# Third to fifth sparse product of a graph network: the dense steps of a block run between the next blocks

## Reference

```python
# layer 0: two graph convolutions (first and second sparse product)
# layer 1: one sum over the edges, then two dense layers with a norm over the nodes
agg = jax.ops.segment_sum(x[src] + edge_feat, dst, num_segments=x.shape[0])
h = (1.0 + epsilon) * x + agg
h = jax.nn.relu(_batchnorm(h @ W1 + b1, g1, beta1))
h = jax.nn.relu(_batchnorm(h @ W2 + b2, g2, beta2))
...
# layer 2: two of these, with a leaky ReLU between them
msg = jax.ops.segment_sum(h[src], dst, num_segments=n_nodes)
h_neigh = (msg + h) / (deg[:, None] + 1.0)
return h_neigh @ W + b
...
# layer 3: three rounds that need max, min, mean and variance over the edges of a node
# between the layers
x = _layernorm(x + layer(x), axis=-1)
```

## Time and profile before

| | |
|---|---|
| median of 3 runs | 3185.71 us (3182.45 to 3189.19) |
| profiled execution, its own time | 3187.43 us |
| its span | 3185.6 us |
| busy in the span | PE 2330.5, PEld 1326.7, DVE 2185.1, ACT 659.8, POOL 1274.1 us |
| third product | 844.06 to 953.8 us of the span |
| fourth | 1014.72 to 1118.9 us |
| fifth | 1142.82 to 1246.1 us |
| layer 3, three rounds | from about 1279 us to the end |

### The profile page before, as it was taken

One profiled execution on the slowest core, in us unless ns is written; L12 is line 12 of the kernel. 1 busy time (PEld: TensorE's weight loads), 2 busy tenths in 40 slices (PEclk: granted clock), 3 DMA queues, 4 the chain that ended last, 5 costly groups with the idle time before them and its releaser, 6 DMA issues.

```text
span 3185.6 us, 49509 instructions
## 1 busy us (share of the span) xinstructions
PE 2330.5 (73%) x11826; PEld 1326.7 (42%) x11873; DVE 2185.1 (69%) x6856; ACT 659.8 (21%) x1425; POOL 1274.1 (40%) x1321
## 2 busy tenths in 40 slices
PE   7999869998896988766566767666667676666681
PEld 3444335674563655433333444333334443333351
DVE  8998777557427244766666787666668876666786
ACT  0345551342103010300000043111111421111112
POOL 4000000000200000577777706777775077777740
PEclk9999989999897999878777789777778887777795
DMA  3123347536641543665565406665663166656521
GB/s 134 62 103 124 145 163 258 182 112 216 210 166 64 194 146 113 199 196 196 196 198 194 145 10 227 194 197 194 195 198 114 60 208 196 197 192 197 193 79 41
DMA packets 151716, 510.46 MB, mean 160 GB/s; under 512 B 32178, under 2 KB 51280, under 8 KB 150720
## 3 DMA queue, kind: packets, MB, share of 16 engines
q1 hardware_dynamic: 94254, 348.65, 31.3%
q0 software_dynamic: 43536, 93.43, 11.1%
q10 hardware_dynamic: 13826, 67.12, 5.2%
HBM read 278.95 MB, written 230.13 MB: 160 GB/s over the span
## 4 chain that ended last, share of the span: by engine, by line
PE 28%; DVE 24%; issue 16%; POOL 14%; DMA 11%; ACT 3%; DVEq 2%; ACTq 0%; POOLq 0%
POOL rows_g L671 14%; PE psum L1680 11%; DMA rows_g<-a_dram,idx_now 9%; PE psum L1620 8%; DVE run L853 4%; DVE run L1158 3%; DVE run L1155 2%; PE psum L1913 2%; DMA at_part<-part_now 2%; PE psum L1629 1%; DVE var_tmp L1097 1%; PE psum L1891 1%; PE psum L1752 1%; DVE hs L1204 1%; PE psum L1761 1%
## 5 line engine op out<-in xcount | busy, mean ns | idle before, releaser
L671 POOL DMA_INDIRECT rows_g<-a_dram,idx_now x1173 | 1138.8, 971 | 974.7 <-DMA a_dram<-g 618.1
L1680 PE MATMUL psum<-hs,slab 128*128 128x384 bf16 x6600 | 1174.2, 340 | 55.5 <-DVE hs L835 52.0
L1680 PEld LDWEIGHTS psum<-hs,slab 128*128 128x128 bf16 x6600 | 672.3, 102 | 581.7 <-issue 189.7
L1155 DVE SCALAR_TENSOR_TENSOR run<-run,mask_pt,rows_g 128x128 f32<-128x128 f32 x1170 | 406.0, 347 | 374.9 <-DMA rows_g<-a_dram,idx_now 330.5
L1158 DVE SCALAR_TENSOR_TENSOR run<-run,mask_pt,rows_g 128x128 f32<-128x128 f32 x1170 | 403.6, 345 | 0.1
L1851 PE MATMUL psum<-identity,std_now 128*128 128x128 f32 x75 | 33.9, 452 | 483.8 <-ACT std_now L1513 483.8
L1620 PE MATMUL psum<-onehot_key,onehot_lane 128*128 128x512 bf16 (+1 forms) x1921 | 347.6, 335 | 10.6 <-issue 8.0
L782 DVE TENSOR_SCALAR onehot_key<-key_row,key_at 128x1600 bf16<-128x1600 f16 x492 | 310.1, 630 | 0.0
L1513 ACT ACTIVATE std_now<-var_now,eps 128x128 f32<-128x128 f32 x75 | 30.1, 401 | 1242.7 <-DVE var_now L1117 1242.7
L1620 PEld LDWEIGHTS psum<-onehot_key,onehot_lane 128*128 128x128 bf16 x1968 | 157.3, 98 | 185.6 <-DVE onehot_key L782 20.3
L1851 PEld LDWEIGHTS psum<-identity,std_now 128*128 128x128 f32 x75 | 13.3, 178 | 509.8 <-ACT std_now L1513 509.3
(11 more groups left out here) (319 smaller groups left out, 2742.0 us busy)
## 6 DMA issues: line engine op xcount, KB each, us to landing
slab<-at_part SPq DMA_DIRECT2D x200, 800.0 KB, 4.6
scan_dram<-run SPq DMA_DIRECT2D x291, 512.0 KB, 2.9
at_part<-part_now ACTq DMA_DIRECT2D x50, 800.0 KB, 4.0
sums_dram<-run ACTq DMA_DIRECT2D x43, 576.0 KB, 2.8
rows_g<-a_dram,idx_now POOLq DMA_INDIRECT x1173
rows_g<-in_attr SPq DMA_DIRECT2D x43, 148.5 KB
a_dram<-g SPq DMA_DIRECT2D x15, 320.0 KB, 2.5
agg<-sel_dram SPq DMA_DIRECT2D x3, 1600.0 KB, 8.4
```

The lines of the kernel that those rows point to most:

```text
L671: nc.gpsimd.indirect_dma_start(rows_g[:, slot, j, :], None, a_dram, bass.IndirectOffsetOnAxis(ap=idx_now[:, slot, j:j + 1], axis=0)).then_ ...
L1155: V.scalar_tensor_tensor(at[:, 0:D], before[:, 0:D], mark, rows, ALU.add, ALU.max).then_inc(s_run, 1)
L1680: T_.matmul(ps[:, 0:3 * D], counts[:, k * P:(k + 1) * P], hs[:, k, at:at + 3, :].rearrange("p s f -> p (s f)"), start=(k == 0), stop=False ...
```

## The change

For the third to fifth product the two phases are put into one loop. `with_products` is the loop of TensorE: after the sums of block b come the transpose of block b-1 and the dense product of block b-2. Bank 3 + r % 3 holds the transpose of block r in its first 128 columns and the product in the next 128; `turned` gets three places (`turned_at`). ScalarE copies the turned block in `copy_turned`, between its other work. VectorE runs `behind(b)` after it has taken block b: the result of block b-3, and what follows it up to the split (`leaky_and_split`) or to the normalised rows (`layer_out`), for one to three blocks behind that. The leaky ReLU, the split and the last norm are now done by blocks of 128 rows, and no longer by groups of five or for all 25 at once. The loops are written out: all 25 blocks of a product are instructions of their own, where before they were three of a loop and four or one outside it. The queue of the loads is not changed.

```diff
@@ -83,6 +83,7 @@
 GT = -(-T // Q)
 RING = 4
 PAIRS = -(-NB // 2)
+FINISHED = {2: 7 * NB, 3: 9 * NB, 4: 11 * NB}
...
+        def turned_at(b):
+            return turned[:, b % 3 // 2, b % 3 % 2 * P:b % 3 % 2 * P + P]
...
-                    in_turn(dve, 3, take)
+                    for b in range(NB + late):
+                        if b < NB:
+                            take(b, b % 3, b // 3)
+                        behind(b)
...
+            def result_of(base, r, take):
+
+                dve.wait_ge(s_mm, base + (r + 1))
+                take(r, bank(3 + r % 3)[:, P:2 * P]).then_inc(s_res, 1)
+                dve.wait_ge(s_res, base + (r + 1))
+
+            def first_hidden(b):
+
+                r = b - 3
+                if r >= 0:
+                    result_of(NB, r, lambda r, ps: V.tensor_scalar(blk(ft, r), ps, cols[:, 0:1], None, ALU.add))
+                    if r % (CB // P) == CB // P - 1 or r == NB - 1:
+                        ins_ = chunk_stats(ft, r // (CB // P))
+                        if r == NB - 1:
+                            step(ins_)
+
             gather_sums(2, plus(edge_sum),
                         lambda b, rows: V.scalar_tensor_tensor(rows, row(x, b), one_eps[:, 0:1], rows,
-                                                               ALU.mult, ALU.add))
+                                                               ALU.mult, ALU.add),
+                        behind=first_hidden, late=3)
             dve.sem_inc(s_rows, 1)
-            for i in range(NCB):
-                for b in range(i * CB // P, min(NB, (i + 1) * CB // P)):
-                    dve.wait_ge(s_mm, NB + (b + 1))
-                    V.tensor_scalar(blk(ft, b), bank(4 + b % 2)[:, 0:D], cols[:, 0:1], None, ALU.add).then_inc(s_res, 1)
-                dve.wait_ge(s_res, NB + (b + 1))
-                last = chunk_stats(ft, i)
-            step(last)
...
-            gather_sums(3, plus(x), times(rdeg))
-            dve.sem_inc(s_rows, 1)
-            results(3 * NB + 7, NB, lambda b, ps: V.tensor_tensor(g[:, b, :], ps[:, 0:D], rows3[:, 1, :], ALU.add))
-            dve.wait_ge(s_res, 4 * NB + 7)
-            for i in range(NG):
-                rows = g[:, GB * i:GB * i + GB, :]
-                V.scalar_tensor_tensor(rows, rows, 0.01, rows, ALU.mult, ALU.max).then_inc(s_group, 1)
-            groups_done[0] += NG
-            dve.wait_ge(s_group, groups_done[0])
-            dve.sem_inc(s_rows, 1)
-            split(3, g, 0)
-            gather_sums(4, plus(g), times(rdeg))
-            dve.sem_inc(s_rows, 1)
-            for b in range(NB):
-                dve.wait_ge(s_mm, 4 * NB + NCB + b + 1)
-                V.tensor_tensor(agg[:, b, :], bank(4 + b % 2)[:, 0:D], rows3[:, 2, :], ALU.add).then_inc(s_res, 1)
-                dve.wait_ge(s_res, 4 * NB + NCB + b + 1)
-                step(V.tensor_tensor(agg[:, b, :], agg[:, b, :], x[:, b, :], ALU.add))
-                last = V.bn_stats(stats[:, b, :], agg[:, b, :])
-            step(last)
-            layer_norm(None, 6)
-            by_groups(normalized(x, agg))
+            ahead = NB // 3 + 1
+
+            def leaky_and_split(b):
+
+                r = b - 3
+                if 0 <= r < NB:
+                    result_of(3 * NB + NCB, r, lambda r, ps: V.tensor_tensor(g[:, r, :], ps, rows3[:, 1, :], ALU.add))
+                    V.scalar_tensor_tensor(g[:, r, :], g[:, r, :], 0.01, g[:, r, :], ALU.mult, ALU.max).then_inc(
+                        s_ln_x, 1)
+                r = b - 4
+                if 0 <= r < NB:
+                    dve.wait_ge(s_ln_hi, ahead + r + 1)
+                    V.tensor_tensor(agg[:, r, :], g[:, r, :], hs[:, r, 3, :], ALU.subtract).then_inc(s_ln_rest, 1)
+                r = b - 5
+                if 0 <= r < NB:
+                    dve.wait_ge(s_ln_mid, ahead + r + 1)
+                    V.tensor_tensor(hs[:, r, 5, :], agg[:, r, :], hs[:, r, 4, :], ALU.subtract).then_inc(s_ln_lo, 1)
+
+            gather_sums(3, plus(x), times(rdeg), behind=leaky_and_split, late=5)
+            dve.wait_ge(s_ln_lo, ahead + NB)
+            dve.sem_inc(s_r1, NG)
+            dve.sem_inc(s_hs, NG)
+            dve.sem_inc(s_rows, 2)
+
+            def layer_out(b):
+
+                r = b - 3
+                if 0 <= r < NB:
+                    result_of(4 * NB + NCB, r, lambda r, ps: V.tensor_tensor(agg[:, r, :], ps, rows3[:, 2, :], ALU.add))
+                    step(V.tensor_tensor(agg[:, r, :], agg[:, r, :], x[:, r, :], ALU.add))
+                    step(V.bn_stats(stats[:, r, :], agg[:, r, :]))
+                    V.bn_aggr(mv[:, r, :], stats[:, r, :]).then_inc(s_ln_stats, 1)
+                r = b - 4
+                if 0 <= r < NB:
+                    dve.wait_ge(s_ln_std, ahead + r + 1)
+                    step(V.reciprocal(rstd[:, r:r + 1], std[:, r:r + 1]))
+                    V.tensor_scalar(x[:, r, :], agg[:, r, :], mv[:, r, 0:1], rstd[:, r:r + 1], ALU.subtract,
+                                    ALU.mult).then_inc(s_ln_x, 1)
+
+            gather_sums(4, plus(g), times(rdeg), behind=layer_out, late=4)
+            dve.wait_ge(s_ln_x, ahead + 2 * NB)
+            dve.sem_inc(s_rows, 3)
...
+            def copy_turned(b, trs, mms):
+
+                act.wait_ge(s_tr, trs + (b + 1))
+                if b >= 3:
+                    act.wait_ge(s_mm, mms + (b - 2))
+                A.copy(turned_at(b), bank(3 + b % 3)[:, 0:P]).then_inc(s_trc, 1)
+
             act.wait_ge(s_sel_copy, NG)
-            in_turn(act, 3, sel_block)
-            turned_blocks(NB, NB, NB, D)
+            for i in range(NB + 2):
+                if i < NB:
+                    sel_block(i, i % 3, i // 3)
+                if i >= 2:
+                    copy_turned(i - 2, NB, NB)
             root_of(8, cstd[:], cmv[:, 1:2], 0)
             act.wait_ge(s_rows, 9)
             for i in range(7):
@@ -1471,10 +1519,28 @@
                              scale=cscale[:, 0:1]).then_inc(s_trc, 1)
             root_of(12, std[:], mv[:, :, 1], 0)
             split(2, x, 0, groups=NG)
-            turned_blocks(2 * NB, 3 * NB, 3 * NB + 7, D)
-            split(3, g, 0, groups=2 * NG)
-            turned_blocks(3 * NB, 4 * NB, 4 * NB + 7, D)
-            root_of(17, std[:], mv[:, :, 1], 0)
+            ahead = NB // 3 + 1
+            for i in range(NB + 3):
+                if i < NB:
+                    copy_turned(i, 2 * NB, 3 * NB + NCB)
+                r = i - 2
+                if 0 <= r < NB:
+                    act.wait_ge(s_ln_x, ahead + r + 1)
+                    A.copy(hs[:, r, 3, :], g[:, r, :]).then_inc(s_ln_hi, 1)
+                r = i - 3
+                if r >= 0:
+                    act.wait_ge(s_ln_rest, ahead + r + 1)
+                    A.copy(hs[:, r, 4, :], agg[:, r, :]).then_inc(s_ln_mid, 1)
+            act.sem_inc(s_hi, NG)
+            act.sem_inc(s_mid, NG)
+            for i in range(NB + 2):
+                if i < NB:
+                    copy_turned(i, 3 * NB, 4 * NB + NCB)
+                r = i - 2
+                if r >= 0:
+                    act.wait_ge(s_ln_stats, ahead + r + 1)
+                    A.activation(std[:, r:r + 1], mv[:, r, 1:2], ACT.Sqrt, bias=eps[:, 0:1]).then_inc(s_ln_std, 1)
+            act.sem_inc(s_std, 1)
...
-                    count_products(pe, [bank(slot)], [3 if c == 2 else 0], slab[slot], range(NB - 1), flag, c, b, slot,
-                                   halves)
+                    count_products(pe, [bank(slot)], [3 if c in (2, 4) else 0], slab[slot], range(NB - 1), flag, c, b,
+                                   slot, halves)
 
                 def first():
                     one(0, 0, 0, n)
@@ -1675,7 +1741,10 @@
             def count_products(pe, banks, ats, counts, ks, flag, c, b, slot=0, halves=None):
                 for k in ks:
                     if halves is not None and k % GB == 0:
-                        pe.wait_ge(s_hs, NG * halves + k // GB + 1)
+                        if c == 4:
+                            pe.wait_ge(s_ln_lo, NB // 3 + 1 + k + GB)
+                        else:
+                            pe.wait_ge(s_hs, NG * halves + k // GB + 1)
...
+            def with_products(c, one, first, trcs, ress, product):
+
+                for b in range(NB + 2):
+                    if b == 0 and first:
+                        first()
+                    elif b < NB:
+                        one(b, b % 3, b // 3)
+                    if 1 <= b <= NB:
+                        r = b - 1
+                        pe.wait_ge(s_fin, FINISHED[c] + 2 * r + 2)
+                        if r >= 3:
+                            pe.wait_ge(s_res, ress + (r - 2))
+                        T_.transpose(bank(3 + r % 3)[:, 0:P], agg[:, r, :], identity[:]).then_inc(s_tr, 1)
+                    if b >= 2:
+                        r = b - 2
+                        pe.wait_ge(s_trc, trcs + (r + 1))
```

(24 more changed lines are left out.)

4 lines of the change are left out of this document (2 added, 2 removed).

## The result

The changed kernel takes 3154.3 us (median of 4 runs, 3151.55 to 3155.27) where the kernel before took 3185.15 on the same chip (4 runs, 3182.45 to 3189.19). The ratio is 0.9901, 95% interval [0.9884, 0.9918], so the change saves 30.9 us.

What follows compares the result with a forecast made beforehand. TensorE alone bounds a product, a chain over all engines the stretch between two. Gains of 6.1, 10.8 and 20.3 us at the three ends, net of the products' cost, sum to 37.2: forecast 3149 us, range 3137 to 3165.

Steps and rivals of the forecast that it cites:

- The price of a product: Third to fifth product: the added transposes and dense products lengthen each by 7.4 us, 22.1 in all.
- The rival by which TensorE pays more: Three products: an f32 pair costs 0.47 us, above the distances between starts, 9.5 us more, 3158 us; chance 0.14.
- lockstep: Products: VectorE and ScalarE set the pace, 5 us a block in two products, 30 us lost, 3179 us; chance 0.04.
- The third's end: After the third product: aggregate 3.6 us after its last sum instead of 17.1; 13.5 gained, 6.1 after the product's cost.
- The fourth's end: Fourth product's end to the fifth's block 0: T + 11.3 instead of T + 29.5, gain 10.8 us after the product's cost.
- T: The end of a product's last sum, about 0.02 us before VectorE starts on the last block.
- The 1.75 us for the clock: Fifth product's first block: its slowdown by the reduced clock, 5.65 us instead of 3.9, was kept in the forecast.
- the last split: After the fourth product: block 24's split ready at T + 8, after five late VectorE turns of 1.35 us.
- The fifth's end: After the fifth product: last `take_g` at T + 16.4 instead of T + 44.1, gain 20.3 us after the product's cost.
- one group of them is now ahead, 1.1 us: T + 6.4 + 10.0: Fifth product's end: with one group ahead, the 11.1 us chain to the last `take_g` takes 10.0 after the last result.
- All after the last `take_g` is left as it was: Behind the fifth product's end: nothing changes, gathers start when `g` is in DRAM, nothing else known to hold them.
- Code loading: Written-out blocks: rival that some 20 more instruction packets cost 2.6 us each, 52 us in all, 3200 us; chance 0.06.

Runs made afterwards that it cites:

- Early slabs: The changed kernel with the fifth product's slabs loaded as places come free in the fourth: ratio 0.9905 to the kernel before, fourth's end 7.49 us against 11.35.
- tail kernel: The changed kernel with layer 3's first transposes and copies between the fifth product's late blocks, dense products in banks 5 to 7: ratio 0.9906 to the kernel before.
- the second pair: The kernel before and the changed kernel, both unedited, profiled again on another chip in the last group: medians differ by 31 us.
- the written-out loops: The kernel before with only TensorE's loops of the third to fifth product written out: 3726.02 us, ratio 0.9999 to the kernel before.

## Why the prediction was right, and where it was off

**The price of a product** was right: 7.54, 7.47 and 7.55 us against 7.4. The distances 0.10 and 0.23, read from the earlier trace rows where the work stood in bunches and from the one f32 matmul in the earlier trace rows, held between bf16 sums as 0.11 and 0.22. The rival by which TensorE pays more is refuted by the table, and lockstep by VectorE's 45 us of 103.

**The third's end** was right: 4.06 us for 3.6, a gain of 13.0 for 13.5.

**The fourth's end** was right in size and in cause: T + 11.1 for T + 11.3, the slab used at T + 5.3 for 5.4, the block at mean clock 0.70. The 1.75 us for the clock took the length of a row (5.65) against 24 distances between starts (3.9); length against length (4.07 in the earlier trace rows) it is 1.6, and 1.7 were measured. Early slabs confirmed that the slab's wait, and with it the clock, is what is left. One part was off without effect: the last split came at T + 5.8, not T + 8, since a late turn of VectorE lasts 0.93 us and not 1.35. Had it been 8 the early slabs would have gained less than they did.

**The fifth's end** is the mis-sized term: 18.28 us against T + 16.4, a gain of 25.8 for 27.7, still inside its bounds (T + 14 to T + 20). The last result was even early (T + 5.9 for 6.4), and the last `x` at T + 7.7 for 8.3. The step that failed is "one group of them is now ahead, 1.1 us: T + 6.4 + 10.0". The group's transposes were ahead, but its copy was not: it stood behind three square roots on ScalarE, and the products of the first group began at 1243.32, T + 7.7, where the step has them at about T + 7.5 (6.4, and 1.1 of the 2.2 us between 1279.08 and 1281.26 in the earlier trace rows). From there the chain took 10.5 us until the last take, against 8.9 from 1281.26 to 1290.20: the half clock, taken by the sum as over after ten transposes, lasted from 1241.6 until about 1248 and covered the five products of the first group (2.50 us) and the transposes of the third group (1.27 for five) as well. The tail kernel, which has the copies between the square roots and no wait of the second group for results, brought this stretch to 14.06 us at full clock, with no idle stretch of TensorE over 1.26 us. It changed both things in one edit, so how the 4.1 us divide between them and the clock is not settled by a run.

**The sum.** The three products with their ends brought 34.8 us for 37.2. The third product started 0.7 us earlier, which is scatter; the stretch between the third's aggregate and the fourth product got 0.8 shorter, which the prediction did not have; and the one from the last take to the first gather got 0.2 longer, and 0.5 in the second pair. What the prediction held unchanged, all after the last `take_g`, cost some 5 us on the mean. The step that failed there is "All after the last `take_g` is left as it was". It named that assumption and was wrong in it, by more than in any term it worked out. That the time still fell well inside the range is due to the range's width of 12 to 16 us: none of its bounds was drawn for this loss.

**Code loading.** The fear was that 20 more packets might each cost something. There are 23 more, and the written-out loops show them to be free: 0.00 to 0.01 us a product. The rule of the Trainium skill, "Runtime: NRT & Kernel Launch", section "Instruction fetch mechanics", by which a taken branch outside the current pages stalls, did not show in these 75 blocks: whether the branches over 50 instructions left those pages no row says, but none of them cost time.

## What to carry to other kernels

Small f32 work put between the matmuls of a stretch that one engine sets is paid in full there, at its distance between starts; it pays off because the same work behind the product costs the chain of waits between the engines, here 17 us at the third product's end for what takes 7.5. When such a phase goes, look at what it had covered: a transfer that was issued at its start, an in-order engine's later work queued behind small steps, and a store that now meets the next one in the queue. Price the half clock behind an idle stretch as part of the wait, for it goes when the wait goes.

## What the runs showed of the hardware

- A wait of TensorE of 2.32 us was followed by a block at mean clock 0.70 (5.75 us for 24 matmuls); with one of 0.27 us in its place the block ran at full clock (4.06). Idle stretches of 1.25 and 0.41 us stood ahead of it both times. At the fifth's end short bursts with idle stretches up to 2.21 us were followed by 6.8 us at 0.53.
- A store of 1600 KB issued 1.2 us ahead on the SyncE queue made the stores of 320 KB behind it land in 5.7 us on the median instead of 2.9; put last it lands in 6.4 itself and leaves them at 3.1.
- The same program takes 3185 us on two of the chips and 3679 and 3725 on two others, while the third to fifth product and their ends are alike to 0.2 us. In 500 us of the third layer the changed kernel moved 163 GB/s on the first chip and 124 on the slowest, as its windows there show (1700 to 2200 us; first chip first). Why was not tried.

```profile
1700.00:2200.00 500.00, 326.89 (x1477) 189.31 (x1477) 362.25 (x1169) 92.17 (x220) 312.38 (x321) 0.80 0.50 163
```

```profile
1700.00:2200.00 500.00, 271.77 (x1198) 157.13 (x1199) 298.29 (x927) 75.10 (x201) 235.10 (x240) 0.75 0.37 124
```
